# Two-layer recurrent block on one core: 32x32 state blocks and a weight split by q, k, v in layer 0 attention, a moved wait in layer 1

## The reference

```python
def body(S, xs):
    qb, kb, vb = xs
    scores = jnp.einsum('bhid,bhjd->bhij', qb, kb) * intra_decay[None]
    o_intra = jnp.einsum('bhij,bhjd->bhid', scores, vb)
    o_inter = jnp.einsum('bhid,bhde->bhie', qb * q_decay[None, :, :, None], S)
    S_new = blk_decay[None, :, None, None] * S + jnp.einsum('bhjd,bhje->bhde', kb * k_decay[None, :, :, None], vb)
    return (S_new, o_intra + o_inter)
...
qkv = (x @ Wqkv + bqkv).reshape(B, N, 3, H, hd)
...
return out @ Wout + bout
```

## Time and profile before

| | |
|---|---|
| median of 3 runs | 2978.14 us (2975.74 to 2980.45) |
| the profiled execution | 2976.12 us |
| its span, first to last instruction | 2974.4 us, 51004 instructions |
| mean granted clock of TensorE | 0.986 of full speed |
| TensorE busy with matmuls | 2845.4 us |
| VectorE, ScalarE, GpSimd busy | 1852.7, 1289.9, 1416.7 us |
| layer 0 attention | from the start to about 574 us |
| layer 1 attention opens | at 1174.63 us |

### The profile page before, as it was taken

One profiled execution on the slowest core, in us unless ns is written; L12 is line 12 of the kernel. 1 busy time (PEld: TensorE's weight loads), 2 busy tenths in 40 slices (PEclk: granted clock), 3 DMA queues, 4 the chain that ended last, 5 costly groups with the idle time before them and its releaser, 6 DMA issues. The chain is left out here.

```text
span 2974.4 us, 51004 instructions
## 1 busy us (share of the span) xinstructions
PE 2845.4 (96%) x19392; PEld 2010.0 (68%) x19392; DVE 1852.7 (62%) x2721; ACT 1289.9 (43%) x2021; POOL 1416.7 (48%) x1003
## 2 busy tenths in 40 slices
PE   6999999799999997899999999999999789999999
PEld 5878788678888886555555555555555278888887
DVE  5656776667777763766666666666666744444444
ACT  3221111266666663355555555555555522222222
...
GB/s 128 89 62 49 58 69 53 36 60 97 85 85 93 97 82 126 103 72 72 72 72 72 71 72 72 76 78 82 76 72 87 95 128 86 90 87 89 87 88 46
DMA packets 124570, 238.89 MB, mean 80 GB/s; under 512 B 13440, under 2 KB 48384, under 8 KB 124416
## 3 DMA queue, kind: packets, MB, share of 16 engines
...
## 5 line engine op out<-in xcount | busy, mean ns | idle before, releaser
L1348 DVE TENSOR_REDUCE l_attn_maxima<-l_attn_ps_max 128x2 f32<-128x1024 f32 x499 | 610.0, 1222 | 221.4 <-PE l_attn_ps_max L1472 217.3
L1319 POOL TENSOR_TENSOR l_attn_summed<-l_attn_summed,stage 128x1024 f32<-128x1024 f32 x248 | 586.2, 2397 | 36.7 <-ACT stage L1257 36.7
L1257 ACT ACTIVATE stage<-l_attn_ps_sc 128x1024 f32<-128x1024 f32 x512 | 497.8, 1030 | 150.1 <-PE l_attn_ps_sc L1459 150.0
L1319 POOL TENSOR_TENSOR l_attn_summed<-stage 128x1024 f32<-128x1024 f32 x124 | 293.7, 2390 | 240.6 <-ACT stage L1257 240.6
L1717 POOL TENSOR_TENSOR l_ffn_ht_lo<-stage,l_ffn_ht_hi 128x512 fp32r<-128x512 f32 x88 | 113.7, 1292 | 413.7 <-ACT l_ffn_ht_hi L1738 413.7
L62 PE MATMUL l_attn_ps_prep<-l_w_tile,l_x_tiles 128*128 128x384 f32 x1440 | 284.9, 346 | 1.6
L71 PE MATMUL l_ffn_ps_fc<-l_w_tile 128*128 128x512 f32 x1024 | 268.2, 405 | 6.6 <-DVE l_w_tile L865 5.0
L1482 PE MATMUL l_attn_ps_y<-stage,l_attn_v 128*32 128x512 f32 x2048 | 272.7, 605 | 1.1 <-ACT stage L1257 1.1
L62 PEld LDWEIGHTS l_attn_ps_prep<-l_w_tile,l_x_tiles 128*128 128x128 f32 x1440 | 246.7, 189 | 34.6 <-issue 14.8
L71 PEld LDWEIGHTS l_ffn_ps_fc<-l_w_tile 128*128 128x128 f32 x1024 | 184.6, 190 | 41.7 <-issue 5.5
L71 PE MATMUL l_ffn_ps_out<-l_ffn_t_proj,l_ffn_ht_hi 128*128 128x512 f32 x512 | 207.0, 404 | 0.0
...
## 6 DMA issues: line engine op xcount, KB each, us to landing
...
```

The lines of the kernel that those rows point to most:

```text
L1257: act.activation(probs[kt % RING][:, hs, :], ps_sc[:, hs, :], ACT.Exp, scale=ATT_SCALE).then_inc(exp_done, 1)
L1319: pool.tensor_tensor(total[:, hs, :], old[:, hs, :], probs[kt % RING][:, hs, :], ALU.add).then_inc(added, 1)
L1348: dve.tensor_reduce(maxima[b][:, j, PAIR * hp:PAIR * hp + PAIR, half:half + 1], pair, AX.X, ALU.max).then_inc(max_read, 1)
```

## The change

- The state is held as 32x32 blocks, `state` 128 x 4 x 32. TensorE's update (L505 after) is 16 matmuls instead of 4, each of one head; the state half of the output (L538 after) is 16 matmuls on the array's diagonal blocks. `own_head` and its making on GpSimd are gone, and VectorE's three passes of 128x512 are two of 128x128.
- On TensorE the state half stands ahead of the wait for `masked_ready`.
- Wqkv is loaded and split by q, k and v (each in two halves); each first projection waits for its own part only. The v split on VectorE goes behind the statistics of chunk 2, the decay tables on ScalarE behind x of chunk 1, the Wout split to the end of tick 1. The waits for decays and masks move to where they are used.
- The sums are stored in tick 12 and loaded back in tick 13.
- In layer 1's prologue TensorE waits for the identity before the first transpose, and for all constants before `turn_max`. GpSimd waits for its own constants at the end of making them.

```diff
                     wq_t = Wqkv.rearrange("(k p) n -> p k n", p=P)
-                    for k in range(KD):
-                        sp.dma_start(raw_q[:, k, :], wq_t[:, k, :]).then_inc(raw_in[k], 16)
+                    for which in (PQ, PK, PV):
+                        sp.dma_start(raw_q[:, :, part(which)], wq_t[:, :, part(which)]).then_inc(raw_in[which], 16)
                     sp.dma_start(raw_o, Wout.rearrange("(k p) n -> p k n", p=P)).then_inc(raw_o_in, 16)
                 for n in pieces_of(t, SUM_FROM, SUMS_PER_TICK):
                     load_piece(n, n % 2, part_done, n - 1)
-                if t == SUM_FROM + PIECES:
+                if t == TERNARY_FROM - 2:
                     sp.wait_ge(sums_done, 2)
                     sp.dma_start(sums_out.rearrange("(p m) -> p m", m=2), sums[:, :]).then_inc(sums_moved, 16)
+                if t == TERNARY_FROM - 1:
                     sp.wait_ge(sums_moved, 16)
...
-                pool.memset(own_head[:, :, :], 1.0).then_inc(iotas, 1)
                 pool.memset(keep[:, :], 1.0).then_inc(iotas, 1)
-                pool.wait_ge(iotas, 6)
+                pool.wait_ge(iotas, 5)
                 pool.memset(keep[:, CPB - 1::CPB], 0.0).then_inc(masks_made, 1)
-                v = own_head[:, :, :].rearrange("p g (h e) -> p g h e", h=HPG)
-                pool.affine_select(out=v, in_=v, compare_op=ALU.is_ge, fill=0.0, base=0,
-                                   pattern=[[0, GROUPS], [-HD, HPG], [0, HD]], channel_multiplier=1).then_inc(iotas, 1)
-                pool.wait_ge(iotas, 7)
-                pool.affine_select(out=v, in_=v, compare_op=ALU.is_ge, fill=0.0, base=HD - 1,
-                                   pattern=[[0, GROUPS], [HD, HPG], [0, HD]], channel_multiplier=-1).then_inc(masks_made, 1)
...
-            def split(k):
-                act.wait_ge(raw_in[k], 16)
-                act.activation(wq_hi[:, k, :], raw_q[:, k, :], ACT.Copy).then_inc(w_hi_made, 1)
+            def split(which):
+                act.wait_ge(raw_in[which], 16)
+                for ks in HALVES:
+                    act.activation(wq_hi[:, ks, part(which)], raw_q[:, ks, part(which)], ACT.Copy).then_inc(w_hi_made, 1)
...
             def tick(t, p):
                 if t == -1:
-                    split(0)
-                    split(1)
+                    split(PQ)
                 if t == 0:
-                    split(2)
-                    split(3)
-                    decay_tables()
-                    act.wait_ge(raw_o_in, 16)
-                    act.activation(wo_hi[:, :, :], raw_o, ACT.Copy).then_inc(w_hi_made, 1)
+                    split(PK)
+                    split(PV)
...
+                if t == 0:
+                    decay_tables()
+                if t == 1:
+                    act.wait_ge(raw_o_in, 16)
+                    act.activation(wo_hi[:, :, :], raw_o, ACT.Copy).then_inc(w_hi_made, 1)
...
-            def split(k):
-                dve.wait_ge(w_hi_made, k + 1)
-                dve.tensor_tensor(wq_lo[:, k, :], raw_q[:, k, :], fp32(wq_hi[:, k, :]), ALU.subtract).then_inc(w_lo_made, 1)
+            def split(which):
+                for n, ks in enumerate(HALVES):
+                    dve.wait_ge(w_hi_made, 2 * which + n + 1)
+                    dve.tensor_tensor(wq_lo[:, ks, part(which)], raw_q[:, ks, part(which)], fp32(wq_hi[:, ks, part(which)]),
+                                      ALU.subtract).then_inc(w_lo_made, 1)
...
                 if isinstance(t, int) and t == -1:
-                    split(0)
-                    split(1)
+                    split(PQ)
                 if isinstance(t, int) and t == 0:
-                    split(2)
-                    split(3)
-                    dve.wait_ge(bias_in, 32)
-                if isinstance(t, int) and t == 1:
-                    dve.wait_ge(w_hi_made, KD + 1)
-                    dve.tensor_tensor(wo_lo[:, :, :], raw_o, fp32(wo_hi[:, :, :]), ALU.subtract).then_inc(w_lo_made, 1)
-                    dve.wait_ge(decays, HEADS + GROUPS + 2)
-                    dve.wait_ge(masks_made, 3)
-                if isinstance(t, int) and t == 0:
+                    split(PK)
                     dve.memset(state[1][:, :, :], 0.0)
                     dve.memset(state[0][:, :, :], 0.0).then_inc(zeroed, 1)
+                    dve.wait_ge(bias_in, 32)
                 if live(t, CHUNKS):
                     evacuate(t, p, PQ)
...
+                    if isinstance(t, int) and t == 1:
+                        dve.wait_ge(decays, HEADS + GROUPS + 2)
...
+                if isinstance(t, int) and t == 0:
+                    split(PV)
...
+                    if isinstance(t, int) and t == 1:
+                        dve.wait_ge(masks_made, 2)
...
+                    kp = keep[:, bass.ds(c, 1)] if not isinstance(c, int) else keep[:, c:c + 1]
+                    need(dve, state_ready, c)
+                    dve.scalar_tensor_tensor(out=state_kept[:, :, :], in0=state[b][:, :, :], scalar=kp,
+                                             in1=blk_decay[:, :].rearrange("p (g a) -> p g a", a=1).to_broadcast([P, GROUPS, HD]),
+                                             op0=ALU.mult, op1=ALU.mult).then_inc(st_step, 1)
                     need(dve, upd_done, c + 1)
-                    kp = keep[:, bass.ds(c, 1)] if not isinstance(c, int) else keep[:, c:c + 1]
-                    dve.scalar_tensor_tensor(out=state_new[:, :, :], in0=ps_state[:, :, :], scalar=kp, in1=own_head[:, :, :],
-                                             op0=ALU.mult, op1=ALU.mult).then_inc(st_step, 1)
-                    need(dve, state_ready, c)
                     need(dve, o_done, c)
-                    dve.scalar_tensor_tensor(out=state[1 - b][:, :, :], in0=state[b][:, :, :], scalar=kp,
-                                             in1=blk_decay[:, :].rearrange("p (g a) -> p g a", a=1).to_broadcast([P, GROUPS, P]),
-                                             op0=ALU.mult, op1=ALU.mult).then_inc(st_step, 1)
-                    need(dve, st_step, 2 * c + 2)
-                    dve.tensor_tensor(state[1 - b][:, :, :], state[1 - b][:, :, :], state_new[:, :, :],
-                                      ALU.add).then_inc(state_ready, 1)
+                    need(dve, st_step, c + 1)
+                    dve.scalar_tensor_tensor(out=state[1 - b][:, :, :], in0=ps_state[:, :, :], scalar=kp, in1=state_kept[:, :, :],
+                                             op0=ALU.mult, op1=ALU.add).then_inc(state_ready, 1)
                     need(dve, ot_hi_ready, c + 1)
                     dve.tensor_tensor(ot_lo[b][:, :, :], ps_o[:, :, :], fp32(ot_hi[b][:, :, :]),
                                       ALU.subtract).then_inc(ot_lo_ready, 1)
+                if isinstance(t, int) and t == 1:
+                    dve.wait_ge(w_hi_made, W_PARTS)
+                    dve.tensor_tensor(wo_lo[:, :, :], raw_o, fp32(wo_hi[:, :, :]), ALU.subtract).then_inc(w_lo_made, 1)
...
-            def project(p, which):
+            def project(t, p, which):
+                if isinstance(t, int) and t == 0:
+                    pe.wait_ge(w_lo_made, 2 * which + 2)
                 w = slice(DIM * which, DIM * which + DIM)
                 three_pass(pe, proj_banks[which][:, :, :].rearrange("p a n -> p (a n)"),
                            lambda k: xt_hi[p][:, k, :], lambda k: xt_lo[p][:, k, :],
@@ -469,15 +474,11 @@
                 q = (p + 1) % 2
                 if isinstance(t, int) and t == -1:
                     pe.wait_ge(made, 4)
-                if isinstance(t, int) and t == 0:
-                    pe.wait_ge(w_lo_made, KD)
-                if isinstance(t, int) and t == 2:
-                    pe.wait_ge(w_lo_made, KD + 1)
...
-                    need(pe, st_step, 2 * c - 1)
+                    need(pe, state_ready, c)
                     for g in range(GROUPS):
-                        gs = slice(P * g, P * g + P)
-                        mm = pe.matmul(ps_state[:, g, :], k_dec[q][:, gs], qkv[q][:, 2 * DIM + P * g:2 * DIM + P * g + P],
-                                       start=True, stop=True)
+                        for h in range(HPG):
+                            own, v = slice(P * g + HD * h, P * g + HD * h + HD), 2 * DIM + P * g + HD * h
+                            mm = pe.matmul(ps_state[HD * h:HD * h + HD, g, :], k_dec[q][:, own], qkv[q][:, v:v + HD],
+                                           start=True, stop=True, skip_group_check=True)
...
+                    if isinstance(t, int) and t == 2:
+                        pe.wait_ge(w_lo_made, W_PARTS)
...
+                    for g in range(GROUPS):
+                        for h in range(HPG):
+                            r = slice(HD * h, HD * h + HD)
+                            pe.matmul(ps_o[r, g, :], state[q][r, g, :], q_dec[q][r, g, :], start=(g == 0), stop=False,
+                                      skip_group_check=True)
```

(6 more changed lines are left out.)

22 lines of the change are left out of this document (12 added, 10 removed).

## The result

The changed kernel takes **2955.68 us** (median of 4 runs, 2952.82 to 2957.25) against 2977.96 us of the kernel before: a ratio of 0.9923 with a 95% interval of 0.9911 to 0.9935, so 19 to 26.5 us less. The forecast was 2957.0. The profiled execution took 2957.25 us, 18.9 less than the profiled one of before, with a span of 2955.5 us.

A forecast was written before the change was run, and what follows sets the result against it. TensorE, busy for 96% of the span, was taken as the bound. Terms -7.4 - 4.8 - 5.9 + 3.2 - 2.5 - 1.1 - 2.7 = -21.2 us took 2978.1 to 2957 us; range about 2950 to 2976.

The forecast's parts named there:

- The ternary ticks, -7.4: Layer 0 attention, sixteen ticks: issuing the state half before the wait for masked scores covers TensorE's wait, -7.4 us.
- 3 instead of 5 passes: VectorE's fewer passes in layer 0 attention, priced at nothing because VectorE works there beside TensorE.
- The exchange, -4.8: Layer 0 attention: storing the sums at tick 12 and loading at tick 13 removes the long 21.40 us tick, -4.8 us.
- The update, -5.9: State update on TensorE: shorter small matmuls, with v then bound by the k evacuation; 0.19 us over 31 ticks, -5.9 us.
- the state half, +3.2: State half of the output as 16 diagonal matmuls: 1.08 us instead of 0.98 over 32 chunks, +3.2 us.
- Rival 1: State update: 32 small records take the pace of large matmuls, +9.6 us instead of -5.9; 2972 us, chance 0.18.
- Rival 2: State half of the output: diagonal tiles in one PSUM bank run one after another, +84 us, 3041 us; chance 0.12.
- The start, -2.5: Kernel start: loading and splitting weights by q, k, v brings first v at 25.2 instead of 29.07 us; -2.5 us net.
- tick 1, -1.1: Tick 1 of layer 0 attention: chunk 0's state half moves ahead of the masking, -1.1 us, its own length.
- Layer 1, -2.7: Opening of layer 1 attention: first projection no longer waits for the constants, -2.7 us (bounds -3.5 and -1.3).
- Rival 3: Start and waits: gains given back by late x, decay tables or L544 still waiting; half of 16 us lost, 2965 us, chance 0.10.

The follow-up runs named there:

- experiment 1: Changed kernel with output halves swapped, masked wait first: 2963.65 us; kernel before with only its state half issued ahead of that wait: 2968.79 us against 2978.58.
- experiment 6: Changed kernel with TensorE's wait for k's evacuation moved from ahead of the v projection to behind it, ahead of the scores: 2952.99 us.
- experiment 5: Changed kernel with the two loops around the state update's small matmuls swapped, so four neighbours use one column tile: 2965.38 us.
- experiment 4: Kernel before with only the start changed (weights loaded and split by q, k, v; decay tables and Wout split moved): 2975.91 us against 2979.36.

## Why the prediction was right, point by point

- **The ternary ticks, -7.4:** right, in size and in cause. The two parts of experiment 1 give +8.0 and -9.8 (-8.3 by the ratio) with the 1 us of tick 1 in them. The sentence that three instructions taken from VectorE's tick make a late L544 less likely carried nothing: the relief is worth nothing, and it is one instruction less and two shorter ones, not three less. The "3 instead of 5 passes" of the sum are two instead of three.
- **The exchange, -4.8:** right; 4.85 in the traces, 4.7 alone (3.3 by the ratio).
- **The update, -5.9, and the state half, +3.2:** right as a sum (-2.7 against -2.4) and each within a tenth of a microsecond a tick. The step that set the k evacuation as the bound was right: v starts 0.06 us after its end. The size of the update itself (0.3 us for the records) was right too (0.26); leaving was set at 0.2 and costs 0.13 where nothing is waited for, as experiment 6 shows. That experiment also shows that this bound has a second one close behind it: without the wait the looped ticks are as long as before, for a reason that stays open.
- **Rival 1** (small matmuls take the pace of large ones) falls: 32 records in 0.26 us. The Trainium skill's rule on the least time between starts, about 25 ns ("TensorE: Matmul & The Clock Gate", section "Wait — 56ns, not 53.3ns?"), would have made it an estimated 0.8 us. Across tiles the trace disagrees (6 to 12 ns); within one tile experiment 5 shows 26 to 32 ns, which agrees.
- **Rival 2** (diagonal tiles of one bank serialise) falls: L538 has 32 records in 1.01 us, the same as L544. The Trainium skill's rule ("TensorEngine Tiling (Array Packing)", Gotcha 1: PSUM Pressure), that different row tiles cannot access the same bank at once, did not show for these tiles, which write different partitions of it. The rival's own working has a slip: a quarter of the overlap is 0.66 us a tick, six rounds' worth of 0.11 and not three.
- **The start, -2.5, and tick 1, -1.1:** the mis-sized term, -0.9 together in the profiled execution, and nearly all of the miss is in the start: 0.0 instead of -2.5. It has two steps. The first is the landing of chunk 2's x, set at 21.4 from the 14.2 us of before: it was issued at 7.48, took 15.4 us and came at 22.94. From there the chain is as forecast (3.74 us to the first v, forecast 3.8), so v starts at 26.68 instead of 25.2, 1.5 us late. The landing of the first weights was set too early as well (9.4, measured 10.88) and moves the first projection from 14.4 to 15.77, but v waits for the x and not for that. The second step is the clock: a stand of 2.8 us was foreseen and priced by the eight slow matmuls of the exchange, 1.4 us, but the whole v projection ran slow, 31.97 - 26.68 = 5.29 us where it had taken 2.86, so 2.4. The same start in two other executions gave -2.7 and -1.3, as experiment 4 says: the toll is paid in some and not in others, and that the -2.5 lies inside what was seen is in part luck.
- **Layer 1, -2.7:** right in kind and a little small: 3.65 alone (interval 0.9 to 6.6), about 3 at the block's end; the wait itself is 2.8, and the rest goes with the clock of this stretch, which no run isolates.
- **Rival 3** (gains given back) is true of the start alone. The profiled execution gained 18.9 us, 2.3 less than the sum, where the rival needs 8 us given back; the median is 22.3 us lower.
